# Router logits in four column tiles, and another order of the steps behind the attention, in a fused two-layer kernel

## The reference

```python
o = o * jax.lax.rsqrt(jnp.mean(o * o, axis=-1, keepdims=True) + eps)   # per head, 16 heads of 32
o = o * jax.nn.silu(g_out.reshape(Bm, Tm, H, DV))
y = o.reshape(Bm, Tm, VAL_DIM) @ o_w.T
x = _layernorm(x + y, axis=-1)

# mixture of 8 experts, two per token, and a shared expert
logits = x @ gate_weight.T                      # 2048 x 512 times 512 x 8
scores = jax.nn.softmax(logits, axis=-1)
topk_w, topk_idx = jax.lax.top_k(scores, TOP_K)
...
sgu = x @ shared_gate_up.T
sact = jax.nn.silu(sgu[:, :Fs]) * sgu[:, Fs:]
y = y + sact @ shared_down.T
```

## Time and profile before

| what | value |
|---|---|
| median of 3 runs | 2700.85 us (2693.25 to 2711.85) |
| profiled execution | 2698.7 us, span 2696.9 us |
| mean granted clock of PE in it | 0.958 |
| busy share of the span | PE 90%, DVE 69%, ACT 48%, POOL 50% |
| PE busy from 617.68 to 649.67 us | 28.72 of 31.99 us |
| PE busy from 649.67 to 680.96 us | 31.24 of 31.29 us |
| PE busy from 680.96 to 718.01 us | 37.00 of 37.05 us |

### The profile page before, as it was taken

The page is one execution under the profiler, slowest core; times in us unless marked ns, Lnnn a source line. Parts: engine busy times, 40 slices in busy tenths (PEclk is TensorE's granted clock), DMA queues, the critical chain, the costliest instruction groups (busy, mean ns, idle before and its releaser), DMA issues.

```text
span 2696.9 us, 33625 instructions
## 1 busy us (share of the span) xinstructions
PE 2416.9 (90%) x11898; PEld 1391.1 (52%) x11898; DVE 1855.0 (69%) x2248; ACT 1281.6 (48%) x2059; POOL 1347.0 (50%) x610
## 2 busy tenths in 40 slices
PE   7887749999999999999488899999999988999998
PEld 2333324444677999865133333333433333678886
DVE  5768875544665666575799889889988988741222
ACT  4444335531234666443657656764675452234433
POOL 0222239850050000340699999999999995122221
PEclk9999869989899999999799899999999999999999
DMA  6464443332064777540464675666577555100000
GB/s 231 144 156 112 127 104 93 91 101 94 13 231 143 271 269 271 196 152 18 127 194 160 188 213 175 201 194 195 172 198 215 195 180 204 45 1 16 1 16 32
DMA packets 251641, 387.11 MB, mean 144 GB/s; under 512 B 131776, under 2 KB 154304, under 8 KB 243808
## 3 DMA queue, kind: packets, MB, share of 16 engines
q1 hardware_dynamic: 232016, 336.76, 38.5%
q0 software_dynamic: 9296, 38.80, 5.8%
q10 hardware_dynamic: 10176, 9.50, 1.0%
HBM read 315.00 MB, written 62.65 MB: 140 GB/s over the span
## 4 chain that ended last, share of the span: by engine, by line
PE 56%; DVE 13%; POOL 10%; issue 9%; DMA 5%; ACT 4%; SPq 2%; ACTq 0%; PEldq 0%; PEld 0%; POOLq 0%; DVEq 0%
PE psum L2143 8%; POOL arena L862 5%; PE psum L2090 5%; PE psum L2324 4%; PE psum L2325 4%; POOL arena L854 3%; DMA arena<-bc_scr 3%; PE psum L3235 2%; PE psum L3035 2%; DVE arena L2787 2%; SPq L2417 2%; PE psum L2297 2%; PE psum L1986 2%; PE psum L2298 2%; PE psum L1988 2%
## 5 line engine op out<-in xcount | busy, mean ns | idle before, releaser
L854 POOL TENSOR_TENSOR arena<-arena 128x2048 f32<-128x2048 f32 x128 | 600.8, 4694 | 111.0 <-DVE arena L1635 74.7
L2143 PE MATMUL psum<-arena,cst 128*128 128x512 f32 x1024 | 501.8, 625 | 92.9 <-POOL arena L862 83.1
L1162 ACT ACTIVATE psum<-arena,negA 128x512 f32<-128x512 f32 x512 | 333.4, 682 | 281.1 <-DVE arena L1650 240.4
L2143 PEld LDWEIGHTS psum<-arena,cst 128*128 128x128 f32 x1024 | 188.4, 195 | 385.6 <-issue 209.8
L1650 DVE TENSOR_TENSOR_SCAN arena<-psum,arena 128x512 f32<-128x512 f32 x256 | 310.8, 1214 | 101.6 <-POOL arena L854 58.8
L862 POOL TENSOR_TENSOR arena<-arena 128x1024 f32<-128x1024 f32 x128 | 323.3, 2526 | 19.3 <-DMA arena<-bc_scr 10.3
L1650 DVE TENSOR_TENSOR_SCAN psum<-psum,arena 128x512 f32<-128x512 f32 x256 | 296.9, 1205 | 0.1
L911 POOL TENSOR_TENSOR arena<-arena 128x512 f32<-128x512 f32 x64 | 87.1, 1361 | 324.8 <-ACT arena L1286 319.3
L2090 PE MATMUL psum<-arena 128*128 128x512 f32 x512 | 231.5, 596 | 1.3 <-PE psum L2090 0.8
L1770 DVE TENSOR_TENSOR r<-arena,r 128x512 fp32r<-128x512 f32 x64 | 46.1, 722 | 237.6 <-ACT r L1291 237.5
L2324 PE MATMUL psum<-r 128*128 128x512 f32 x512 | 201.5, 394 | 3.6 <-ACT arena L1286 2.5
(11 more groups left out here) (392 smaller groups left out, 4868.5 us busy)
## 6 DMA issues: line engine op xcount, KB each, us to landing
arena<-bc_scr SPq DMA_DIRECT2D x256, 512.0 KB, 4.8
arena<-w_exp SPq DMA_DIRECT2D x23, 1408.0 KB, 6.1
arena<-in_gu SPq DMA_DIRECT2D x44, 512.0 KB, 4.8
arena<-in_inw SPq DMA_DIRECT2D x32, 512.0 KB, 3.5
arena<-in_dn SPq DMA_DIRECT2D x31, 512.0 KB, 6.9
x_scr<-arena SPq DMA_DIRECT2D x19, 512.0 KB, 6.0
arena<-in_x SPq DMA_DIRECT2D x8, 1024.0 KB, 10.1
w_exp<-in_gu SPq DMA_DIRECT2D x16, 512.0 KB, 7.4
```

The source lines that it names most:

```text
L854: nc.gpsimd.tensor_tensor(dB[:, at:at + 2], du[:, j:j + 2].unsqueeze(1).broadcast_to([P, 2, 2, T]), BR[:, q % 2].unsqueeze(2).broadcast_to ...
L1162: nc.scalar.activation(psum[:, bank], dt[:, b % 2, j + t], ACT.Exp, scale=negA2[:, at:at + 1]).then_inc(s["da_ok"], 1)
L2143: ins = mm(psum[:, t], ident, dB[:, k % NSLOT, t], start=False, stop=(n == NS - 1), skip_group_check=True)
```

## The change

The logits now take the 8 gate columns as weights and 128 tokens as the moving operand. The four token tiles of a block go to four column tiles of the array, partitions 0, 32, 64 and 96 of psum bank 6 (logits_rows_pe). ACT copies this 128x128 result to memory (logits_copy_act), and one transposition on PE brings tokens back to partitions (logits_turn_pe). route_dve reads 8 of every 32 columns of that. The semaphore lg_mm now counts the transposition; lr_mm and lr_ok are new.

The order of PE's loop changes too. Values-back blocks stand behind groups 0 and 2 (1 and 2 before). The variance of block b - 1 stands behind group 0 of round b, and the spreading of its rows behind group 1. Behind the last group come mean squares, the logits' matmuls, spread_roots, the logits' transposition and then the mean. On DVE, times_inverse stands ahead of center_dve. In the mixture the transposition of block 3 stands behind down(0).

```diff
@@ logits
-        def logits_pe(pe, b):
+        def logits_rows_pe(pe, b):
             pe.wait_ge(s["ln_done"], b + 1)
             if b:
                 pe.wait_ge(s["rt_d"], b)
-            for t in range(4):
-                for k in range(KT):
-                    ins = nc.tensor.matmul(psum[:, 6, t * E:(t + 1) * E], x[:, k, b * T + t * P:b * T + (t + 1) * P], gw[:, k],
+            for k in range(KT):
+                for r, t in enumerate(colq):
+                    ins = nc.tensor.matmul(psum[32 * r:32 * r + E, 6, 0:P], gw[:, k], x[:, k, b * T + P * r:b * T + P * r + P],
                                            start=(k == 0), stop=(k == KT - 1))
-            ins.then_inc(s["lg_mm"], 1)
+            ins.then_inc(s["lr_mm"], 1)
+
+        def logits_copy_act(act, b):
+            wait(act, "lr_mm", b + 1)
+            if b:
+                act.wait_ge(s["lg_mm"], b)
+            nc.scalar.copy(lgt, psum[:, 6, 0:P]).then_inc(s["lr_ok"], 1)
+
+        def logits_turn_pe(pe, b):
+            wait(pe, "lr_ok", b + 1)
+            nc.tensor.transpose(psum[:, 6, P:2 * P], lgt, ident).then_inc(s["lg_mm"], 1)
@@ route_dve
-            ch.link(v.tensor_copy(r_lg, psum[:, 6, 0:32].rearrange("p (t e) -> p t e", t=4)))
+            ch.link(v.tensor_copy(r_lg, psum[:, 6, P:2 * P].rearrange("p (t e) -> p t e", t=4)[:, :, 0:E]))
@@ moe_act, behind round_h(n)
+                if n == 1:
+                    logits_copy_act(act, B - 1)
@@ moe_pe
                 if n == 1:
-                    logits_pe(pe, B - 1)
+                    logits_rows_pe(pe, B - 1)
...
                 if n:
                     down(n - 1)
+                if n == 1:
+                    logits_turn_pe(pe, B - 1)
@@ ACT's loop
                 o_square(b + 1)
                 o_root(b + 1)
+                if b:
+                    logits_copy_act(act, b - 1)
                 square_act(act, b)
                 root_rows_act(act, b)
             act.wait_ge(s["ln_done"], 1)
             nc.scalar.copy(xh[0], x[:, :, 0:T]).then_inc(s["xh_ok"], 1)
+            logits_copy_act(act, B - 2)
@@ DVE's loop
                 inverse_root(b + 1)
+                times_inverse(b + 1)
                 center_dve(dve, b)
-                times_inverse(b + 1)
@@ PE's loop
                     ins.then_inc(s["pm_ok"], 1)
+                    if m in (0, 2) and b + 1 < B:
+                        values_back(b + 1, m)
+                        values_back(b + 1, m + 1)
                     if m == 0 and b:
+                        var_rows_pe(pe, b - 1)
+                    if m == 1 and b:
                         spread_rows_pe(pe, b - 1)
-                    if m in (1, 2) and b + 1 < B:
-                        values_back(b + 1, 2 * m - 2)
-                        values_back(b + 1, 2 * m - 1)
                 pe.sem_inc(s["y_mm"], 1)
                 if b + 1 < B:
                     mean_squares(b + 1)
-                else:
-                    logits_pe(pe, b - 1)
+                if b:
+                    logits_rows_pe(pe, b - 1)
+                if b + 1 < B:
+                    pe.wait_ge(s["x_ok"], b + 1)
+                    spread_roots(b + 1)
+                if b:
+                    logits_turn_pe(pe, b - 1)
                 mean_pe(pe, b)
-                if b + 1 < B:
-                    spread_roots(b + 1)
-                    if b:
-                        logits_pe(pe, b - 1)
-                    var_rows_pe(pe, b)
```

More of the change, by code:

```diff
@@ L292, in build @@
                 ("pm_ok", "kc_ok", 2 * B), ("o_re", "g_ev", 4 * B), ("ob_mm", "g1_mm", 16 * B), ("ln_b", "pt_ok", B), ("hs_ok", "kc_mm", 2 * B),
+                ("lr_mm", "ab_used", 2 + 2 * B), ("lr_ok", "k_out", 32 * B),
                 ("w_in0", "m_in", 128 * B), ("w_in1", "t_out", 128 * B), ("xr_in0", "xload", 32 + 96),
@@ L350, in build @@
         ytk = view(39936, 2048, "p (u c) -> p u c", u=4)
+        lgt = view(20480, P)
         rt = view(37632, 256)
```

## The result

| what | before | changed |
|---|---|---|
| median of 20 runs each | 2703.4 us (2692.3 to 2716.8) | 2687.5 us (2678.2 to 2698.4) |
| ratio | | 0.9942, 95% interval 0.9930 to 0.9953 |
| profiled execution, span | 2696.9 us | 2685.9 us |

What follows compares the result with a forecast made beforehand. PE's executed work and clock were taken as the bound; -9.4 - 3.2 + 0.75 + 1.6 + 1.0 + 1.6 - 11.4 = -19.0 us, with one fall left called -16.5, giving 2684.3 us from 2700.85; range 2670 to 2699.

Steps and rivals of the forecast that it cites:

- Logits: Four logits blocks on PE: each falls from 3.67 to 1.05 us, saving 10.5 us.
- Transposition: One new PE transposition per logits block, 0.28 us each, 1.1 us in all.
- Wait for the squares: PE's wait for ACT's squares ahead of the variance: 3.2 us go, 0.75 us come in round 3.
- What is late next: New PE waits: reciprocal 1.6 us in round 0, 0.5 each in rounds 1 and 2; residual 1.6 before last mean.
- The clock: Half-clock time between first output projection and mixture: 11.4 us saved at full clock, less 2.7 for one fall left.
- five falls: Half-clock stretches: round changes 2.7, 1.6 and 1.6 us, last mean 3.1, first down block 2.4.
- Does it reach the end: Gate and up weight transfer issued at 766.02: it moves with PE, so the gain is not swallowed.
- (a): Rival: clock falls as before at round changes and last mean; 9.0 us lost, 10 gained, 2691; chance 0.17.
- (c): Rival: PE stays at 1.2 GHz through the rounds, from 618 to 718; +39 us, 2740; chance 0.03.
- (d): Rival: logits' column tiles don't run side by side, 3.67 us per block stay; near -2 us, 2699; chance 0.04.
- (b): Rival: gain swallowed in later stretches, priced at one 10.3 us transfer; 6 us gained, 2695; chance 0.10.
- (e): Rival: over 1% faster, later half-clock stretches fall out 10 us better by chance; 2670; chance 0.08.

Runs made afterwards that it cites:

- version with covered waits: Changed kernel with a quarter of the mean ahead of spreading roots, and block 3's residual ahead of split_dn(0); ratios to the kernel before 0.9908, 0.9919; stretch 100.5 us.
- order-only: Changed kernel with the old logits put back, without copy and transposition; ratio to the kernel before 0.9976, stretch 114.9 us.
- logits-only: Kernel before, in its old order, with the new logits, copy and transposition; ratio 0.9970, stretch 112.4 us.
- two shifts: Kernel before with four or two extra heavy passes, overwritten, ahead of round 1's last projection group; stretches 126.5 and 124.6 us.
- four pieces: Kernel before with the old logits of blocks 0 to 2 cut into four pieces of 8 passes; ratio 1.0021, stretch 124.5 us.
- shift of one step: Kernel before with two extra heavy passes, overwritten, ahead of round 1's last projection group; stretch 124.6 us.

## Why the prediction was right

The time was forecast at 2684.3 us for a gain of 16.5 us; 2687.5 and 15.9 came, since the median before moved to 2703.4 with more runs. That the gain hit within 0.6 us is partly luck: its own interval spans six. The steps, with what the changed kernel's first profile measured:

- *Logits*: 1.05 us foreseen, 1.06; in the mixture it is 0.99 from start to start. The estimate from the span model of the Trainium skill (TensorE: Matmul & The Clock Gate, Part 3), 0.55, was not borne out, as the row of mean squares had said. A pass with 8-column weights takes 273 ns like one with 32. Term right, 10.5 us gained.
- *Transposition*: 0.28 each foreseen, 0.16 and 0.17 in rounds 1 and 2 (648.24 to 648.40), 0.33 ahead of the last mean; in the mixture it ran beside its neighbours. 0.4 us better in all.
- *Wait for the squares*: gone, with 0.89 against 0.75 in round 3.
- *What is late next*: 1.63 (1.6 foreseen), 0.75 twice (0.5 each) and 1.58 ahead of the last mean (1.6). The mis-sized one is the 0.5. VectorE's reciprocal ends 2.56 us behind the start of the mean squares, as foreseen, but PE goes on 0.15 later (646.98, 647.13), and the new logits start 0.1 us sooner than foreseen, so PE stands at the wait earlier. The version with covered waits shows them to be real time: covered, they come back as 4.7 us together with the last fall.
- *The clock*: five falls worth 11.4 us before, one left of 5.40 - 3.60 = 1.8. I had left one of 2.7. For rounds 1 and 2 the order-only and logits-only runs show that neither half does this alone: without the order a 2.2 us wait is followed by the fall, without the short logits the logits are. The falls behind the last mean and in the mixture went with either half.
- *Not in the sum*: these terms, as measured, make some 17 of the 18.1 us. Mean and next group in one piece take 6.97 to 7.06 us where two apart take 7.26, which is part of the rest.
- *Does it reach the end*: yes. The entry behind the transfer moved by 17.3 us. The ranks (725.61, behind transpositions that began at 724.92) waited at most 0.25 us for the routing.
- *Rivals*: (a) happened at one place, in two profiles of three, and cost 1.8 us where it priced 9.0; (c) did not show in any profile; (d) is refuted by 1.06 us. (b) is open at 2 us. (e) did not come.

The reason given was right in mechanism for the logits' own time, the waits, and the three falls of the rounds. For the other two it was too simple. I had tied four of the five falls to the long logits; with the new order and the old logits only those of rounds 1 and 2 came, where light blocks stand on both sides. The 5.5 us of the other two were gained as forecast, but that the short logits are their cause is not shown.

## What to carry to other kernels

Price a cheap-looking instruction block twice: by its own duration, and by what the granted clock does to the heavy work behind it; here the second was more than half of the gain (9.6 of 18.1 us). Before shortening a block, list what it hides: with short logits alone two waits of 2.23 us came out from under them, each with slow work behind it, and the new order on top gave another 7 to 9 us of the stretch (112.4 against 105.1 and 103.5). A wait that remains can be covered with a piece of the next long step, cut by k.

## What the runs showed of the hardware that I had not expected

Matmuls of 128 columns in four column tiles take the same 273 ns, and a block of 32 takes 0.90 to 1.06 us, 28 to 33 ns a pass, with 8 columns of weights as with 32, though the weight load itself took 90 ns against 110.

Waits and blocks of light passes were both followed by half clock here. A wait of 2.23 or 3.22 us with 2 to 3 us of tiled passes around it was followed by half clock in each of eleven cases (nine of 3.22, two of 2.23, over all profiles), a wait of 1.63 us in one of four, the two of 0.39 and 1.19 us ahead of the last mean in one of three, and 0.92 or 1.85 us of 8-column passes never. An uncut block of 3.7 us went both ways.

Different executions mostly meet the clock alike, but not always. Seven profiles (three of the kernel before, its two shifts, logits only, four pieces) run the same passes up to the first wait of 3.22 us. The slow group behind it took 5.54 to 5.80 us in six of them, and 4.26 in the seventh, the shift of one step. So a few profiles of one kernel can look like a law where they are alike by place, and the changed kernel showed three different outcomes.
